# A linear-attention kernel whose system matrix is kept by column block and stored at once, with the chunk lists of all engines redrawn

## What is computed

```python
x = x + attention(layernorm(x))          # the stage that the change touches
x = x + soft_mixture(layernorm(x))       # 1024 slots, w1, gelu, w2

# attention, per batch, with C = 128:
q, k, v = x @ Wq + bq, x @ Wk + bk, x @ Wv + bv
k = k / max(norm(k), 1e-12)
alpha, beta = sigmoid(x @ Wa + ba), sigmoid(x @ Wb + bb)
gate = sigmoid(x @ Wg + bg)
def step(S, t):
    S = S @ (a_t * (I - b_t * k_t k_t^T)) + b_t * v_t k_t^T
    o_t = (q_t @ S) * gate_t
y = o @ Wo + bo
```

## Time and profile before

| what | us |
|---|---|
| three runs | 1237.17, 1241.47, 1233.4 |
| their median | 1237.17 |
| the profiled execution | 1239.12 |
| its span in the trace | 1237.3 |
| interval between two Mrep loads, undisturbed pair | 54.25 / 2 = 27.12 |
| mean of twelve such intervals | 27.65 |
| attention, until VectorE begins the maxima | about 509 |

### The profile page before, as it was taken

The page is one execution under the profiler, slowest core; times in us unless marked ns, Lnnn a source line. Parts: engine busy times, 40 slices in busy tenths (PEclk is TensorE's granted clock), DMA queues, the critical chain, the costliest instruction groups (busy, mean ns, idle before and its releaser), DMA issues.

```text
span 1237.3 us, 27045 instructions
## 1 busy us (share of the span) xinstructions
PE 1130.7 (91%) x8600; PEld 861.7 (70%) x8600; DVE 936.0 (76%) x2195; ACT 735.5 (59%) x1385; POOL 305.6 (25%) x373
## 2 busy tenths in 40 slices
PE   4589888889898987899999999999999999999998
PEld 2367776777677766458678568688468688477687
DVE  4678787888777764799757799767798766998665
ACT  3435555556555543568766378765478755487854
POOL 2536555455555551100002000002000012000012
PEclk9689999999999998999999999999999999999999
DMA  5112223322222224323238111237020337000155
GB/s 183 36 36 63 70 75 92 99 70 69 73 73 69 69 81 104 94 70 63 63 73 162 47 35 35 74 77 162 32 49 21 86 80 150 26 1 1 18 108 131
DMA packets 179119, 90.36 MB, mean 73 GB/s; under 512 B 117280, under 2 KB 170528, under 8 KB 179040
## 3 DMA queue, kind: packets, MB, share of 16 engines
q1 hardware_dynamic: 171984, 71.74, 24.5%
q0 software_dynamic: 5792, 17.05, 4.8%
q10 hardware_dynamic: 1264, 0.53, 0.2%
HBM read 38.42 MB, written 25.69 MB: 52 GB/s over the span
## 4 chain that ended last, share of the span: by engine, by line
PE 58%; DVE 16%; issue 12%; ACT 6%; DMA 5%; POOL 1%; SPq 1%; DVEq 0%; ACTq 0%; POOLq 0%
PE m_wide L1998 14%; PE m_wide L1881 8%; PE m_wide L1975 7%; PE m_wide L1961 7%; DMA Mrep<-M_dram 5%; DVE m_Dm L1581 3%; PE a_bank L1216 3%; DVE m_El L1589 2%; PE m_wide L1986 2%; ACT m_Eh L1764 2%; DVE cmax L1552 2%; PE m_wide L1935 2%; PE a_bank L1180 2%; PE a_bank L1090 1%; ACT kh_ L894 1%
## 5 line engine op out<-in xcount | busy, mean ns | idle before, releaser
L1519 POOL DMA_DIRECT2D out_dram<-m_o x64 | 35.4, 553 | 627.3 <-DVE m_o L1703 624.5
L1935 PE MATMUL m_wide<-m_X,m_Eh 128*128 128x257 f16 (+1 forms) x1024 | 171.5, 273 | 2.6 <-DVE m_El L1589 2.3
L1881 PE MATMUL m_wide<-seT,XT 128*128 128x512 f16 x672 | 147.3, 379 | 0.9 <-issue 0.8
L1998 PE MATMUL m_wide<-m_Ph,m_Th 128*128 128x257 f16 x512 | 140.4, 274 | 4.3 <-DVE m_Pl L1628 4.3
L1935 PE MATMUL m_wide<-m_X,m_El 128*128 128x257 f16 (+1 forms) x512 | 139.7, 273 | 0.0
L1998 PE MATMUL m_wide<-m_Ph,m_Tl 128*128 128x257 f16 x512 | 139.4, 272 | 0.0
L1998 PE MATMUL m_wide<-m_Pl,m_Th 128*128 128x257 f16 x512 | 139.1, 272 | 0.0
L1881 PEld LDWEIGHTS m_wide<-seT,XT 128*128 (+1 forms) x672 | 65.5, 98 | 78.6 <-ACT L L1737 1.5
L1935 PEld LDWEIGHTS m_wide<-m_X,m_Eh 128*128 128x128 f16 x1024 | 99.2, 98 | 20.7 <-DVE m_El L1589 3.8
L1737 ACT COPY L<-m_wide 128x512 f32<-128x512 f32 (+1 forms) x112 | 65.1, 584 | 78.5 <-PE m_wide L1881 77.6
L1757 ACT ACTIVATE m_E<-m_Dm,m_eshift 128x512 f32<-128x512 f32 x128 | 92.5, 722 | 23.5 <-DVE m_Dm L1581 22.5
(11 more groups left out here) (197 smaller groups left out, 2702.9 us busy)
## 6 DMA issues: line engine op xcount, KB each, us to landing
L<-in_L_attn_x_dram SPq DMA_DIRECT2D x16, 512.0 KB, 6.8
Mrep<-M_dram SPq DMA_DIRECT2D x32, 256.0 KB
x_dram<-x SPq DMA_DIRECT2D x16, 512.0 KB, 6.4
m_X<-X_dram SPq DMA_DIRECT2D x128, 64.0 KB, 1.8
m_x1t<-x_dram POOLq DMA_DIRECT2D x32, 256.0 KB, 3.5
out_dram<-m_o POOLq DMA_DIRECT2D x64, 128.0 KB, 2.5
X_dram<-Xh SPq DMA_DIRECT2D x16, 256.0 KB, 2.3
X_dram<-Xl SPq DMA_DIRECT2D x16, 256.0 KB, 2.3
```

The source lines that it names most:

```text
L1881: last = pe.matmul(lg[t % 4], XT[:, sx * KD + k, bass.ds((4 * g + t) * P, P)], seT[:, ss, k, z * HS:(z + 1) * HS], start=(c == 0), stop=(c ...
L1935: last = pe.matmul(acc[v][q], e[t % 4][:, qs], X[:, sx, bass.ds(4 * g + t, 1), 0:XW].rearrange("q a n -> q (a n)"), start=first and e is E ...
L1998: last = pe.matmul(co[p], a, pp[:, e, 0:XW], start=(c == 0), stop=(c == 3 * NS - 1))
```

## The change

1. M is kept by column block: [128, 8 blocks, 4 batches, 16] in place of [128, 4 batches, 128]. VectorE writes it in runs of 16 elements, and the cuts read it so.
2. One store sends all of M to DRAM (256 KB, runs of 64 floats) in place of eight stores of the diagonal blocks (4 KB each). M_dram has rows to spare, so that the diagonal blocks can be read with one stride. The loads into Mrep are as large as before.
3. POOL makes a copy of the quarter of M that the last doubling reads (`half_cut`, Mhalf), in the layout that PE reads.
4. On SP the store of Xl moves from behind the stores of M into the next step, behind the loads of Mrep.
5. The order in `step` is new on all engines. The third doubling with its matmuls and copies, and the updates behind it, are in the same step as the first two. On DVE the four state updates and OT are put between columns, the statistics of x behind them.

The diff, cut to its core (of the written-out orders only a part of DVE's is shown):

```diff
-        M = two("M", [P, B, P])
+        M = two("M", [P, NBK, B, BS])
+        Mhalf = two("Mhalf", [HP, B, HP])
...
             def blocks_out(c, q):
                 sp.wait_ge(M_ok, c + 1)
-                for e in range(NBK):
-                    sp.dma_start(M_dram[e],
-                                 M[q][e * BS:(e + 1) * BS, :, e * BS:(e + 1) * BS]).then_inc(M_out, 16)
+                sp.dma_start(M_dram[0:NBK * P * B * BS].rearrange("(e p f) -> p e f", e=NBK, p=P),
+                             M[q][:, :, :, :].rearrange("p e b t -> p e (b t)")).then_inc(M_out, 16)
 
             def blocks_in(c):
-                out, used = value(sp, 16 * NBK * (c + 1)), value(sp, c)
+                out, used = value(sp, 16 * (c + 1)), value(sp, c)
                 sp.wait_ge(M_out, out)
                 if later(c, 1):
                     sp.wait_ge(base_ok, used)
                 for rows_in, s in ((Mrep_in, 0), (Mrep_late, HROWS)):
                     sp.dma_start(Mrep[:, s:s + HROWS, :, :].rearrange("p s b t -> p (s b t)"),
-                                 M_dram[:, s:s + HROWS].rearrange("e (a s) b t -> e a (s b t)", a=1)
+                                 M_dram.rearrange("(e a f) -> e a f", e=NBK, a=1)
+                                 [:, :, s * B * BS:(s + HROWS) * B * BS]
                                  .broadcast_to([NBK, BS, HROWS * B * BS])).then_inc(rows_in, 16)
...
                 if live(i + 2):
                     blocks_in(i + 2)
+                if live(i - 1) and not (isinstance(i, int) and i == NCH - 1):
+                    store_low(i - 1)
...
-                if live(i):
+                if isinstance(i, int) and i == NCH - 2:
                     store_low(i)
-                if isinstance(i, int) and i == NCH - 2:
                     load_XT0(XT0_PARTS[0], XT0_PARTS[1])
 
-            steps(sp, step)
+            steps(sp, step, first=1)
+            store_low(NCH - 1)
             load_XT0(XT0_PARTS[1], NCH)
...
                 pool.wait_ge(M_ok, c + 1)
                 at = C_MASK + n * P
-                pool.tensor_tensor(moff[q][:, n], M[q][:, :, :], over_batches(const[:, at:at + P]), ALU.mult)\
+                pool.tensor_tensor(moff[q][:, n].rearrange("p b (e t) -> p b e t", t=BS),
+                                   M[q][:, :, :, :].rearrange("p e b t -> p b e t"),
+                                   const[:, at:at + P].rearrange("p (a e t) -> p a e t", a=1, t=BS)
+                                   .broadcast_to([P, B, NBK, BS]), ALU.mult)\
                     .then_inc(moff_ok, 1)
+
+            def half_cut(c, q):
+                pool.wait_ge(M_ok, c + 1)
+                pool.tensor_tensor(Mhalf[q][:, :, :].rearrange("p b (e t) -> p b e t", t=BS),
+                                   M[q][0:HP, NBK // 2:, :, :].rearrange("p e b t -> p b e t"),
+                                   pool_zeros[0:HP, :].rearrange("p (b e t) -> p b e t", e=1, t=1)
+                                   .broadcast_to([HP, B, NBK // 2, BS]), ALU.add).then_inc(moff_ok, 1)
...
                 for s in range(BS - 1):
                     if live(i + 2):
                         product(i + 2, s)
+                    if live(i + 2):
+                        column(i + 2, s)
+                    if s == 4:
+                        if live(i + 3) and at != -2:
+                            biases(i + 3, r, 3)
                     if s == 6:
                         if live(i + 3) and at != -2:
-                            biases(i + 3, r, 3)
-                    if live(i + 2):
-                        column(i + 2, s)
-                    if s == 0:
-                        if live(i + 1):
-                            doubling(i + 1, r, 2)
-                    if s == 7:
-                        if live(i + 3) and at != -2:
                             biases(i + 3, r, 1)
-                    if s == 10:
+                    if s == 8:
                         if live(i + 1):
                             weights(i + 1, r)
                     if s == 10:
-                        if live(i + 4):
-                            statistics_in(i + 4, q, 0)
-                            statistics_in(i + 4, q, 1)
+                        if live(i + 1) and live(i + 2):
+                            next_state(i + 1, r, 0)
+                            next_state(i + 1, r, 1)
+                    if s == 11:
+                        if live(i + 1) and live(i + 2):
+                            next_state(i + 1, r, 2)
+                            next_state(i + 1, r, 3)
+                    if s == 12:
+                        if live(i + 1):
+                            gated(i + 1, r)
                 if live(i + 2):
                     columns_done(i + 2)
-                if live(i + 1):
-                    gated(i + 1, r)
+                if live(i + 4):
+                    statistics_in(i + 4, q, 0)
+                    statistics_in(i + 4, q, 1)
...
             def products(c, q, n):
-                turned, made = value(pe, NLV * c + n + 1), value(pe, NCUT * c + NCUT - n if n < NCUT else c + 1)
+                turned, made = value(pe, NLV * c + n + 1), value(pe, NLV * c + (NCUT - n if n < NCUT else NLV))
                 pe.wait_ge(pool_consts, 1)
                 pe.wait_ge(ZT_ok, turned)
-                pe.wait_ge(moff_ok if n < NCUT else M_ok, made)
+                pe.wait_ge(moff_ok, made)
                 for b in range(B):
                     bs = slice(b * HP, (b + 1) * HP)
                     if n < NCUT:
                         last = pe.matmul(bank[4][:, bs], moff[q][:, n, b, :], ZT[:, bs], start=True, stop=True)
                     else:
-                        last = pe.matmul(bank[4][HP:, bs], M[q][0:HP, b, HP:], ZT[0:HP, bs], start=True, stop=True)
+                        last = pe.matmul(bank[4][HP:, bs], Mhalf[q][:, b, :], ZT[0:HP, bs], start=True, stop=True)
                 last.then_inc(P1T_ps, 1)
 
...
```

197 lines of the change are left out of this document (98 added, 99 removed).

## The result

The changed kernel takes 1188.16 us (median of 4 runs, 1187.25 to 1189.11) against 1236.23 for the kernel before on the same chip: ratio 0.9606, 95% interval 0.9580 to 0.9632. The forecast was 1191 us. In a later comparison the ratio came to 0.9603 (0.9570 to 0.9637). All ratios are of undisturbed executions: one of the six of experiment 7 (3995 us) and one of the kernel before (1249.7 us) are left out. The profiled execution took 1187.25 us, its span 1185.4.

What follows compares the result with a forecast made beforehand. VectorE and TensorE were taken as nearly full, with Mrep arriving late. Loop 9.1, spreading 1.3, doublings 9.2 + 3.5, hand-overs 0.2, lock 0.7, dips 0.3 gave a 24.3 us period; 46.7 us saved gave 1191 us, range 1170 to 1221.

Steps and rivals of the forecast that it cites:

- Column loop: VectorE's loop of products and columns after Mrep lands: 8.55 us before, 9.1 us per period forecast.
- Doublings: Three doublings of Z between column loops, through PE, ACT and DVE: 4.6, 4.6 and 3.5 us per period.
- Hand-overs: Passing work between engines along the period's chain: 0.2 us per period.
- The lock: VectorE operations with two SBUF inputs and POOL operations exclude each other: 0.7 us added per period, bounds 0 and 2.6.
- Clock dips: Drops of the granted clock: 0.3 us added per period, half of the 0.53 before.
- The trip: M's way through DRAM into Mrep: 13.8 us before, 7.9 forecast (6.7 to 11.3), just hidden behind VectorE's work.
- Its bound is near 22: TensorE's work per period, estimated as 24.1 busy us less some 0.2 for each of about ten group ends.
- rival A: VectorE's work alone sets the period, POOL and VectorE pass without blocking: 22.9 us, 1170 us in all; chance 0.12.
- Start-up: Time before chunk 1, said to be set by weight preparation on VectorE, which stays: gain 0.
- The tail: Last column loop, where VectorE waits 2.69 us for scores: updates made a step earlier were to gain 2.5 us.
- Rival C: POOL's operations slide into the column loop and block VectorE: period 29.4 us, about 1262 us in all; chance 0.07.
- who waits gets the next turn: When VectorE and POOL operations exclude each other, the waiting engine runs next; no separate size given.

Runs made afterwards that it cites:

- experiment 7: Changed kernel with M on VectorE behind the first two decay scans and guard made from one input tensor: 1182.69 us, ratio 0.9552.
- experiment 6: Changed kernel with M on VectorE behind the first two decay scans instead of ahead of them: 1184.35 us, ratio 0.9560.
- experiment 1: Kernel before with the single store, M by column block, Mhalf and Xl's store behind the Mrep load, old order of computation: 1210.22 us, ratio 0.9757.
- experiment 3: Kernel before with only Xl's store moved behind the next Mrep load; eight stores, old M layout and old order: 1207.63 us, ratio 0.9748.
- experiment 2: Changed kernel with eight stores of one diagonal block each in place of the single M store: 1190.99 us, ratio 0.9611.
- experiment 8: Changed kernel with M behind the first two decay scans and no guard, the variance taking its floor from a constant: 1182.85 us, ratio 0.9553.
- experiment 12: The changed kernel run once more without edits, against the kernel before: 1189.87 us, ratio 0.9603.
- experiment 11: Changed kernel with four more POOL cuts per chunk (the first cut made five times), some beside the column loop: 1248.06 us, ratio 1.0072.

## Why the prediction was right, and where it was only lucky

**The total.** 1191.0 against 1188.2, well inside 1170 to 1221, and the likeliest case was the one that came: intervals of 24.13 us against 24.3, Mrep no longer waited for. Twelve intervals gave 42.2 us, where 40.2 were forecast. Outside them it was partly luck. In the two traces the start gained 9.95 us where 4.0 were forecast, and the tail -0.3 where 2.5 were: 51.9 us in all against 46.7. The medians differ by 48.1 only, because the profiled execution of the kernel before was 2.9 above its median and that of the changed kernel 0.9 below.

**The period's terms.** Column loop 9.1: measured 9.0 (244.88 to 253.89). Spreading 1.3: 1.27. Doublings 4.6, 4.6 and 3.5: 4.97 (from the end of the spreading at 255.41 to 260.38), 4.36 (236.17 to 240.53) and 3.81 (240.53 to 244.34), 0.4 over. Hand-overs 0.2: 0.25 from the loop to the spreading and 0.54 from the last doubling to the loop, 0.8. The lock 0.7: guard takes 0.63 us, against some 0.15 for the variance, which wasn't held, and this costs nothing: its removal gained nothing on top of experiment 6, and in the changed kernel the last doubling starts at 244.34, when its sums are just ready (244.30). Clock dips 0.3: none. So 23.3 became 24.1 by doublings and hand-overs, and the 1.0 us that I had added for lock and dips made up for it. The sum is right by two errors that cancel, which is luck. One of the prediction's own additions is off too: POOL's run of "some 9.2 us" is 2.36 + 4 x 1.27 + 0.7 = 8.1 by its rows. It took 8.8 with the time lost beside Xl (234.94 to 243.77), and so ended 1.1 us ahead of the loop, which is why the half cut never touched the first product.

**The trip.** Forecast 7.9 us, "just hidden" behind 8.5 to 9: it was 7.0 (M done at 235.6, the load issued at 238.24, 4.35 for its landing), with 2.3 to spare. The store of 256-byte runs landed in 2.6 us where 3.0 were taken, against 2.3 for the same bytes in 512-byte runs. The mechanism was right but its parts were not weighed: the text takes the eight issues of 5.09 us and the wait for Xl together. Experiments 1 and 3 show that in the old order Xl's store alone carried it, and that the new layout of M, Mhalf and the single store together added nothing measurable. In the new order experiment 2 shows this of the single store; the layout and Mhalf weren't taken out there.

**"Its bound is near 22", of TensorE.** This step failed. With nearly no gaps left TensorE is busy for 23.56 us of an interval in the changed kernel and for 23.34 in experiment 6. Taking 0.2 us off for the end of every group that a gap follows was too much: before, 24.1 were shown, so the whole correction was 0.5 to 0.8, not 2. TensorE's queue is therefore part of the chain now, and experiment 8 shows a saving of VectorE's turning into a wait for it. This left rival A (22.9) less room than the 0.12 that it got.

**Start-up, forecast 0, gained.** Mrep's first issue of the window comes 9.95 us earlier, where the two intervals ahead of it were given 4.0 and the start nothing. One part is the lock again, VectorE's timeline of the kernel after in the start-up, beside the earlier trace rows:

```profile
61.60 2.27 DVE L710 TENSOR_TENSOR w1s<-L,w1s 128x2048 f16<-128x2048 f32 x1
```

It took 4.01 us before, beside a POOL residual; now POOL is idle when it starts and kTg behind it waits instead (3.17 us), 1.7 us less in a stretch of which the prediction says that VectorE's weight preparation sets it. Some 3 us come with the move of Xl's store alone: in experiment 3, in the old order and with w1s at 4.27, this issue comes at 124.46. The rest wasn't tested, and in the second trace of the changed kernel (experiment 12) it comes at 118.91, so about a microsecond of it is chance.

**The tail, forecast 2.5, gave nothing.** Behind the last Mrep issue the time is 0.3 us longer. VectorE's timeline of the last column loop, and the window around it, beside the earlier trace rows:

```profile
420.57 0.69 DVE L641 TENSOR_TENSOR PT<-a_bank,gamb_ 128x512 f32<-128x512 f32 x1 [2.88 <-PE a_bank L1216]
```

```profile
413.50:421.00 7.50, 6.29 (x28) 5.80 (x28) 4.04 (x20) 4.08 (x7) 0.00 (x0) 0.56 0.84 172
```

The wait of 2.69 us that the new order was to remove is there with 2.88. The step that failed is "the updates of that chunk will have been made a step earlier": in both kernels they start half a microsecond after the last doubling (465.39 after 464.92, 413.57 after 413.10), with the scores behind them. In the middle of the stage the same four groups from the updates to the scores are recorded with 1.06, 0.66, 1.15 and 1.06 us and PT doesn't wait; here they take 2.08, 1.12, 1.92 and 1.59, 2.8 us more in all, which is the wait. The granted clock is 0.56 in this stretch, so mostly at the lower of its two levels (1.2 and 2.4 GHz), and it was 0.57 in the same stretch before (465 to 473). I had read the wait as a matter of order; that the clock makes it is argued from these rows, and no run tested it.

**Rival C, the lock.** It didn't occur, but experiment 11 shows that its price was about right: 5.1 us of POOL work more gave 3.4 us per interval and lost the whole gain. The step "who waits gets the next turn" holds there, with one VectorE operation between two of POOL, but not in the start-up of experiment 1, where three POOL operations passed a waiting one.

## What to carry to other kernels

Ahead of redrawing layouts, look in an issuing queue for a wait that stands in front of a load on the critical path: moving one store behind that load gave 2.5 of the 3.9% here. Cures of one stall need not add, and here they didn't; try each alone before keeping the costly one. And once no engine shows a long wait, an operation saved on one engine can come back as a wait for the other, as in experiment 8: check first whether the chain changes engines behind it, and keep POOL's operations on 128x512 out of VectorE's chains of tiny dependent operations.

## What the runs showed of the hardware

- An operation of VectorE with a single SBUF input (TENSOR_SCALAR, 128x4, float32) waited for POOL just as one with two did: 0.57 against 0.58 us median, about 0.15 where nothing holds it (var). The rule that two inputs are needed, which I had used, was too narrow.
- Beside back-to-back POOL operations of 1.27 us one VectorE operation got in behind each in experiment 11: four dependent products and columns took 1.13, 1.32, 1.31 and 0.54 us. In experiment 1 a larger one (128x2048) got no turn during three of them and took 7.02 us instead of 2.27.
- A store of 256 KB in runs of 256 bytes landed in 2.6 us, in runs of 512 bytes in 2.3; both are small beside what a store takes that is queued behind the two Mrep loads: 6.6 us for x1's (512 KB), and 5.7 for Xl's (256 KB) in the changed kernel, where it was 2.3.
- The clock's dips are gone along with TensorE's gaps, which I had expected by half: granted 0.98 over the twelve intervals before, 1.00 after, with TensorE busy for 88% and 97% of them. In experiments 1 and 3 it was 1.00 as well, in experiment 11 it was 0.98 again.
